# Gated cross-attention on one core: GpSimd's row-sum adds moved behind the lower halves, and its power for the reciprocal root

## The reference

```python
memory_proj = einsum('bme,de->bmd', memory, W_mem)
scores = einsum('bnd,bmd->bnm', hidden_states, memory_proj) / sqrt(D)
attn = softmax(scores, axis=-1)
memory_context = einsum('bnm,bmd->bnd', attn, memory_proj)
gate_input = concatenate([hidden_states, memory_context], axis=-1)
gate = sigmoid(einsum('bnf,df->bnd', gate_input, W_gate) + b_gate)
fused = hidden_states + gate * memory_context
return fused * rsqrt(mean(square(fused), axis=-1) + 1e-6) * norm_w
```

## Time and profile before

| | |
|---|---|
| median of 3 runs | 561.19 us (560.53 to 563.08) |
| the profiled execution's own time | 562.44 us |
| its span, first to last instruction | 560.6 us |
| mean granted TensorE clock | 0.992 |
| busy: TensorE, VectorE | 541.7 us, 503.4 us |
| busy: ScalarE, GpSimd | 336.2 us, 134.1 us |

### The profile page before, as it was taken

One profiled execution on the slowest core, in us unless ns is written; L12 is line 12 of the kernel. 1 busy time (PEld: TensorE's weight loads), 2 busy tenths in 40 slices (PEclk: granted clock), 3 DMA queues, 4 the chain that ended last, 5 costly groups with the idle time before them and its releaser, 6 DMA issues.

```text
span 560.6 us, 9004 instructions
## 1 busy us (share of the span) xinstructions
PE 541.7 (97%) x2432; PEld 438.8 (78%) x2432; DVE 503.4 (90%) x847; ACT 336.2 (60%) x633; POOL 134.1 (24%) x102
## 2 busy tenths in 40 slices
PE   8999999999999999999999999999999999999992
PEld 7777888878887788878888788887888778887871
DVE  4879959999899998899998998999988999889966
ACT  4676646665567646576366665666565864667534
POOL 0005600244003520055001440025300451005600
PEclk9999999999999999999999999999999999999988
DMA  9965371520683117711385115841088212100033
GB/s 226 260 127 83 90 132 50 98 73 18 148 176 97 37 50 136 167 68 37 98 163 104 56 37 134 171 114 40 0 170 177 75 37 99 52 23 20 0 114 112
DMA packets 184338, 54.25 MB, mean 97 GB/s; under 512 B 161528, under 2 KB 174848, under 8 KB 184320
## 3 DMA queue, kind: packets, MB, share of 16 engines
q1 hardware_dynamic: 183792, 53.52, 40.9%
q10 hardware_dynamic: 528, 0.52, 0.3%
HBM read 45.63 MB, written 8.39 MB: 96 GB/s over the span
## 4 chain that ended last, share of the span: by engine, by line
PE 66%; DVE 17%; issue 10%; SPq 3%; ACT 2%; DMA 2%; ACTq 0%; DVEq 0%
PE bank L357 14%; PE bank L358 13%; PE bank L359 13%; PE bank L524 7%; PE bank L525 7%; PE bank L526 7%; DVE p_lo L838 5%; DVE s L879 3%; DVE fused L984 2%; DVE fused L991 2%; DVE gate L905 2%; ACT fused L696 2%; DVE gate L934 2%; DMA fused<-in_L_xattn_W_gate_dram 2%; SPq L249 2%
## 5 line engine op out<-in xcount | busy, mean ns | idle before, releaser
L1155 POOL TENSOR_TENSOR psum_rows<-psum_rows,p_tmp 128x512 f32<-128x512 f32 (+1 forms) x88 | 122.5, 1392 | 85.4 <-ACT p_tmp L673 84.3
L838 DVE TENSOR_TENSOR p_lo<-p_tmp,p_hi 128x512 fp32r<-128x512 f32 (+1 forms) x104 | 92.3, 889 | 5.5 <-ACT p_hi L635 5.4
L673 ACT ACTIVATE p_tmp<-s 128x512 f32<-128x512 f32 (+1 forms) x104 | 65.2, 628 | 45.1 <-DVE s L879 44.5
L1155 POOL TENSOR_TENSOR psum_rows<-p_tmp 128x512 f32<-128x512 f32 x8 | 10.8, 1354 | 309.4 <-ACT p_tmp L673 309.4
L357 PE MATMUL bank<-q_hi,mt_hi 128*128 128x512 f32 (+1 forms) x208 | 81.7, 393 | 0.0
L358 PE MATMUL bank<-q_lo,mt_hi 128*128 128x512 f32 (+1 forms) x208 | 81.2, 390 | 0.0
L359 PE MATMUL bank<-q_hi,mt_lo 128*128 128x512 f32 (+1 forms) x208 | 81.1, 390 | 0.0
L525 PE MATMUL bank<-p_lo,mem_hi 128*128 128x512 f32 (+1 forms) x208 | 81.0, 389 | 0.0
L524 PE MATMUL bank<-p_hi,mem_hi 128*128 128x512 f32 (+1 forms) x208 | 81.0, 389 | 0.0
L526 PE MATMUL bank<-p_hi,mem_lo 128*128 128x512 f32 (+1 forms) x208 | 80.9, 389 | 0.0
L635 ACT ACTIVATE s<-bank 128x512 f32<-128x512 f32 (+1 forms) x104 | 62.0, 597 | 19.5 <-PE bank L359 19.1
(11 more groups left out here) (93 smaller groups left out, 1057.6 us busy)
## 6 DMA issues: line engine op xcount, KB each, us to landing
mem_raw<-in_ctx_dram SPq DMA_DIRECT2D x48, 256.0 KB, 3.0
mem_blocks<-in_ctx_dram SPq DMA_DIRECT2D x64, 136.0 KB
x_again<-in_x_dram SPq DMA_DIRECT2D x32, 256.0 KB, 2.6
out_dram<-fused SPq DMA_DIRECT2D x32, 256.0 KB, 2.1
x_raw<-in_x_dram SPq DMA_DIRECT2D x112, 64.0 KB, 2.1
mem_blocks<-in_ctx_dram SPq DMA_DIRECT2D x56, 64.0 KB, 2.0
x_raw<-in_x_dram SPq DMA_DIRECT2D x4, 256.0 KB, 4.7
gate<-in_L_xattn_W_gate_dram SPq DMA_DIRECT2D x2, 512.0 KB, 6.1
```

The lines of the kernel that those rows point to most:

```text
L673: nc.scalar.activation(p_tmp[0:r, t % TMP_RING, :], s[0:r, t, :], ACT.Exp, scale=float(D) ** -0.5).then_inc(exp_done, 1)
L838: return nc.vector.tensor_tensor(dst, src, hi.bitcast(F32), ALU.subtract)
L1155: nc.gpsimd.tensor_tensor(psum_rows[0:r, :], a, p_tmp[0:r, t % TMP_RING, :], ALU.add).then_inc(p_added, 1)
```

## The change

GpSimd's add of a tile waits for `p_has_lo`, VectorE's lower half of the same tile, where it waited for `exp_done`. The eleven operations of `rms` leave VectorE. GpSimd makes the reciprocal root in three operations on 128x4: times 1/512, plus epsilon, to the power -0.5, each waiting for the one ahead by a semaphore. VectorE waits for `rms_done` at the same place of its order. Three constant tiles are set at the start.

```diff
@@ scalar, tail
-            act.wait_ge(newton, NEWTON_OPS * B)
+            act.wait_ge(rms_done, B)
@@ vector
-            def rms(b):
...
-                dve.wait_ge(squares_done, NT * (b + 1))
-                link(nc.vector.tensor_scalar(mean_sq[:, :], sq_sum[:, :], 1.0 / D, EPS, ALU.mult, ALU.add))
-                link(nc.vector.tensor_scalar(r_rms[:, :].bitcast(I32), mean_sq[:, :].bitcast(I32), -0.5, RSQRT_MAGIC,
-                                             ALU.mult, ALU.add))
-                for _ in range(NEWTON_STEPS):
-                    link(nc.vector.tensor_tensor(nw_a[:, :], r_rms[:, :], mean_sq[:, :], ALU.mult))
-                    link(nc.vector.scalar_tensor_tensor(nw_b[:, :], nw_a[:, :], -0.5, r_rms[:, :], ALU.mult, ALU.mult))
-                    link(nc.vector.scalar_tensor_tensor(r_rms[:, :], nw_b[:, :], 1.5, r_rms[:, :], ALU.add, ALU.mult))
...
-                    rms(b - 1)
+
+                    dve.wait_ge(rms_done, b)
                     for j in range(NT):
                         output(b - 1, j)
...
-            rms(B - 1)
-
+
+            dve.wait_ge(rms_done, B)
@@ gpsimd
-                pool.wait_ge(exp_done, MT * b + t + 1)
+                pool.wait_ge(p_has_lo, MT * b + t + 1)
...
+            def rms(b):
+
+                pool.wait_ge(squares_done, NT * (b + 1))
+                nc.gpsimd.tensor_tensor(mean_sq[:, :], sq_sum[:, :], one_in_d[:, :], ALU.mult).then_inc(mean_done, 1)
+                pool.wait_ge(mean_done, b + 1)
+                nc.gpsimd.tensor_tensor(mean_sq[:, :], mean_sq[:, :], eps_rows[:, :], ALU.add).then_inc(guarded, 1)
+                pool.wait_ge(guarded, b + 1)
+                nc.gpsimd.tensor_tensor(r_rms[:, :], mean_sq[:, :], minus_half[:, :], ALU.pow).then_inc(rms_done, 1)
...
             with pool.Fori(1, B) as b:
                 for t in range(1, MT):
                     add_p(b, t, False)
+                rms(b - 1)
+            rms(B - 1)
```

More of the change, by code:

```diff
@@ L41 @@
 EPS = 1e-6
-RSQRT_MAGIC = float(0x5F3759DF)
-NEWTON_STEPS = 3
 def xattn_kernel(nc: bass.Bass, x, mem, w, wg, b_gate, norm_w, out):
@@ L123, in xattn_kernel @@
         r_rms = sb("r_rms", [P, NT])
-        nw_a = sb("nw_a", [P, NT])
-        nw_b = sb("nw_b", [P, NT])
+        minus_half = sb("minus_half", [P, NT])
+        one_in_d = sb("one_in_d", [P, NT])
+        eps_rows = sb("eps_rows", [P, NT])
         w_raw = x_again[:, :, :].rearrange("p a (k c) -> p (a k) c", c=C)
@@ L184, in xattn_kernel @@
         z_done, gated, fused_done = sem("z_done"), sem("gated"), sem("fused_done")
-        newton, out_done = sem("newton"), sem("out_done")
+        mean_done, guarded, rms_done, out_done = sem("mean_done"), sem("guarded"), sem("rms_done"), sem("out_done")
+        ready_half = sem("ready_half")
         normed, tail_done = sem("normed"), sem("tail_done")
         p_added = sem("p_added")
-        NEWTON_OPS = 2 + 3 * NEWTON_STEPS
         WT, WG2T, WG1T, V = range(0, 2), range(2, 6), range(6, 10), range(10, 12)
@@ L1155, in add_p @@
                 nc.gpsimd.tensor_tensor(psum_rows[0:r, :], a, p_tmp[0:r, t % TMP_RING, :], ALU.add).then_inc(p_added, 1)
+            def rms(b):
[5 more added lines that the diff above has]
+                nc.gpsimd.tensor_tensor(r_rms[:, :], mean_sq[:, :], minus_half[:, :], ALU.pow).then_inc(rms_done, 1)
             nc.gpsimd.memset(ident[:, :], 0.0).then_inc(cleared, 1)
+            nc.gpsimd.memset(minus_half[:, :], -0.5).then_inc(ready_half, 1)
+            nc.gpsimd.memset(one_in_d[:, :], 1.0 / D).then_inc(ready_half, 1)
+            nc.gpsimd.memset(eps_rows[:, :], EPS).then_inc(ready_half, 1)
+            pool.wait_ge(ready_half, 3)
             pool.wait_ge(cleared, 1)
```

## The result

**The changed kernel takes 586.12 us** (median of 4 runs, 585.18 to 587.80), against 561.28 us before (median of 4, 560.53 to 563.08). The ratio is 1.0437, with a 95% interval of 1.0412 to 1.0462: 4.4% slower. The forecast was 577.4 with a range of 563 to 586; the result lies 8.7 us above the forecast, at the upper edge of the range and 0.1 us past it. The profiled execution took 587.80 us with a span of 586.0 (562.44 and 560.6 before), and its mean granted clock fell from 0.992 to 0.963.

The account below looks back on a forecast made before the run. The prediction took TensorE, busy for 97% of the span, as the bound. Its terms, 6 x 1.1 + 2.6 - 1.0 + 8.0 = +16.2 us on the median of 561.19, gave 577.4 us, range 563 to 586.

Parts of the forecast that it names:

- The walk: VectorE's steps from `p_lo(0)` to `p_lo(12)`: 31.0 us in sum against 29.7, `p_lo(12)` ending 0.8 us later.
- The waits: VectorE before its outputs: 1.5 us for GpSimd's last add plus 1.2 for the root, idle some 2.7 us.
- the lead: End of the batch: VectorE finishes `mt_lo` of pair 0 only 0.46 us ahead of TensorE's scores.
- 6 x 1.1: Batches 1 to 6: scores start at 212.8 instead of 211.72, +1.1 us for each.
- The clock: TensorE's 2.3 us gap before the scores halves its clock in five of six batches, 1.6 us each: +8.0 us.
- The last batch: No x transposes between lower halves; `u_lo(0)` at 539.4 instead of 536.78, TensorE waiting for it: +2.6 us.
- The tail: No GpSimd adds there; ScalarE's 2.3 us wait for the root becomes about 1.3: -1.0 us.
- B: Rival: the clock holds, the same sum without 8.0: 569.4 us; chance 0.27.
- C: Rival: faster, small operations cost 0.3 us in all and adds follow at 0.07: 557.3 us; chance 0.07.
- D: Rival: slow power, three operations taking 3 us cost 14.4 more over eight places: 592 us; chance 0.10.
- E: Rival: no change, B's case with about half of C's savings: 560 to 564 us; chance 0.06.

Follow-up runs that it names:

- e3_filled_gap: Changed kernel plus eleven wide matmuls with unused results in TensorE's gap before the scores: 574.23 us, ratio 1.0238.
- e2_adds_only: Kernel before with only GpSimd's adds moved behind the lower halves, root still on VectorE in eleven operations: 586.36 us, ratio 1.0448.
- e4_root_first: Changed kernel with GpSimd making the root ahead of the last tile's add: 579.31 us, ratio 1.0320.
- e13_product_for_power: Changed kernel with a product in place of the power, so the output is scaled wrongly: 577.01 us, ratio 1.0283.
- e1_root_only: Changed kernel with the adds again behind their exponentials, so only the root moves to GpSimd: 560.35 us, ratio 0.9981.
- e6_shift_ahead: Changed kernel with VectorE's shift of tile t+3 ahead of gate times context, add x and `mem_lo`: 558.27 us, ratio 0.9932.
- e5_outputs_late: Changed kernel with VectorE's wait for the root and the four outputs moved behind `q_lo` and `mt_lo`: 562.83 us, ratio 1.0015.
- e8_early_adds_outputs_late: Changed kernel with adds again behind their exponentials and the outputs moved behind `q_lo` and `mt_lo`: 575.35 us, ratio 1.0236.

## Why the prediction was right and wrong

**The walk: right in its sum, in part by luck.** The step-by-step sum gave 31.0 us between the ends of `p_lo(0)` and `p_lo(12)`; it took 30.94. The places were right in the main: lower halves of tiles 1 to 5 at 0.68 to 0.69, gate times context at 1006 ns in the mean (788 before), `p_lo(12)` at 1.44. The steps of tiles 7 and 8 took the 2.00 of the sum, but their lower halves 0.87 and 0.86 and not 1.3: they began later under the add. One lower half that I had blocked, `p_lo(10)`, ran free in 0.66, and its step took 1.20 instead of 2.00; the one of tile 11, behind add x, took 1.78 and its step 3.40 instead of 2.60. The two errors cancel to a hundredth, which is luck. VectorE and GpSimd at that place:

```profile
204.88 0.66 DVE L836 TENSOR_TENSOR p_lo<-p_tmp,p_hi 128x512 fp32r<-128x512 f32 x1
...
204.50 2.19 POOL L1134 TENSOR_TENSOR psum_rows<-psum_rows,p_tmp 128x512 f32<-128x512 f32 x1 [1.09 <-DVE p_lo L836]
```

Tile 9's add has an earlier start in its record than `p_lo(10)`, and yet the add is the one that took longer, 2.19 instead of 1.29, and so in each batch of the loop; the next add follows 0.08 us behind it and takes 1.62. Add x did not grow (946 against 948): in a batch it was blocked twice before (1.13 and 1.47 us) and is blocked twice now (1.48 and 1.15).

**The waits: right in place, the root too small and the lead too large.** Outputs 3.03 us behind `p_lo(12)`, forecast 2.7. Mean and guard took 0.20 each, as VectorE's small operations had suggested, but the power 1.02, not 0.4. And VectorE's lead over TensorE was not 0.46 us: the scores started 4.96 us behind the first output before and 4.66 now, when nothing but `mt_lo` holds them, so the lead was 0.30. The outputs come 1.70 us later in each batch, less 0.30 makes 1.40, or 8.4 over six; with the clock held up (`e3_filled_gap`) the loop was 9.2 us longer than before, and the 0.8 between the two have no row. "6 x 1.1" was 6.6.

**The clock: right in kind, the term that failed most in size.** "In five of six gaps, 1.6 us each", +8.0. It fell in six of six, and in three of them for 6.83 us instead of 3.41. The price of one short fall was right (some 1.5 us); that the term came to 12.7 us in the traces, 11.9 between the medians, is the sixth fall and the three long ones. I had priced eight matmuls at the low level, from the one fall in the trace of before; that fall was 3.41 us of a stretch, and nothing told me that a longer gap may bring two.

**The rest.** The last batch: +2.6 forecast, +2.6 measured, by luck. `p_lo(12)` came 0.6 us later instead of 2.0, and the outputs 2.0 us further behind it than before instead of 0.6. There the adds fall behind: five run back to back for 9.59 us, ScalarE waits for them with its exponentials (18.7 us in 26 over the run) and VectorE once for `p_hi`, 2.46 us; its outputs come 4.08 us behind the lower half. The tail gained 0.5, not 1.0: the power again. Against the spans the forecast of 16.2 is 9.2 short: 2.6 in the waits, 4.7 in the clock, 0.5 in the tail and 1.4 at the start, which was in no step.

**The rivals.** B (the clock holds, 569.4) fell with the first trace; the filled gap gives what it would have cost, 574.2, which is 4.8 above its price. The Trainium skill (TensorE: Matmul & The Clock Gate, Why this matters for your kernels) would have let only longer gaps throttle; the trace disagrees, gaps of 1.8 to 2.8 us had a fall at 24 of 24 boundaries, in the changed kernel, `e2_adds_only`, `e4_root_first` and `e13_product_for_power`. C would have needed a root of 0.3 us; with three operations of 0.20 (`e13_product_for_power`) the kernel still took 577. D (a slow power) was true in kind and small: three operations in 1.58 us instead of 1.2, not 3. E never came near.

**What the prediction missed altogether.** It charged the second edit with the wait for the last add. The run with the adds alone refutes this: the add stops VectorE's own root in the same way, so the first edit is the whole loss, and the second is worth 0.2% to the good when it stands alone. I had looked for blocked operations among those of 512 columns only.

## What to carry to other kernels

An add on GpSimd was not free beside VectorE in any order here: choose where it starts by the two or three VectorE operations behind it, and put those that read only one SBUF tensor there. One such swap took back more than the two edits had lost, and it did best with the adds left where they were. Before the last operation of a chain is handed to another engine, ask what that engine must finish first. And where TensorE is the bound, keep its gaps short even at the price of useless matmuls: here six gaps of 2.7 us went with 9 us of delay and 12 more of clock. When a result moves back in the program, look at its store: what stands behind it in the DMA queue moves too.

## What was unexpected in the hardware

- **The lock does not ask for size.** VectorE's product of 128x4 took 1.15 us instead of 0.16 while GpSimd's add ran. The other way, GpSimd's 128x4 addition took 0.74 instead of 0.20 beside VectorE's last lower half in `e1_root_only`. The Trainium skill (SBUF — State Buffer, SBUF: two separate sides) describes a lock for the whole instruction, which goes to the one that starts first; these rows agree with the whole instruction and show that four columns are enough. Who gets it does not always follow the starts in the records: tile 9's add began 0.38 us ahead of `p_lo(10)` and took 0.9 us longer than alone, while the lower half took no longer. Why is open.
- **The power** costs 1.02 us on 128x4 on GpSimd, a product or a sum 0.20. Its first call took as long as the other seven.
- **The clock fell at every boundary with a gap of 1.8 to 2.8 us** behind the weighted sums, and at none with 0.13 to 0.26 (`e3_filled_gap`) or 0.45 to 0.54 us (`e6_shift_ahead`) of idle. At another place, ahead of the transposes of `col_max` and behind matmuls on 128 rows, `e5_outputs_late` and `e8_early_adds_outputs_late` have ten more gaps. Those of 0.8 to 1.71 us had no fall, those of 1.89 and 2.28 us had one:

```profile
377.32 0.65 PE L442 MATMUL bank<-ident,col_max 128*128 128x128 f32 x4 [1.71 <-DVE col_max L869]
...
446.32 0.65 PE L442 MATMUL bank<-ident,col_max 128*128 128x128 f32 x4 [1.89 <-DVE col_max L869]
```

  Behind the first of these two the granted clock was 1.00 (377 to 382 us), behind the second 0.72 (446 to 452). The length of the gap alone does not decide it: the earlier trace rows have a fall behind eight one-column matmuls and 0.40 us of idle, and in the last batch of `e4_root_first` one came with 1.57 us of idle ahead of such matmuls. Each fall in the loop lasted 3.41 or 6.83 us; which of the two came, the traces don't explain.
